# The last two slot tiles of two routed expert layers reach the tokens by matrix products instead of gathers

## The reference

```
# L1: top 2 of softmax + bias, with a shared expert beside
comb = sum_c weights[c] * one_hot(idx[c])               # [512, 8]
routed = sum_e comb[:, e] * (swiglu((x@w1[e]+b1[e]) * (x@w3[e]+b3[e])) @ w2[e] + b2[e])
out = routed + swiglu((x@sw1+sb1) * (x@sw3+sb3)) @ sw2 + sb2
# L2: top 2 of the logits, gates renormalised over the two, hidden width 1024
out = sum_e comb[:, e] * (relu(x@W1[e]+b1[e]) @ W2[e] + b2[e])
```

## Time and profile before

| | us |
|---|---|
| median of 3 timed runs | 2891.98 (2891.62 to 2898.47) |
| the profiled execution | 2884.38 |
| its span, first to last instruction | 2882.6 |
| TensorE busy | 2647.0 (92%) |
| VectorE (DVE) busy | 1643.5 (57%) |
| ScalarE (ACT) busy | 1114.2 (39%) |
| GpSimd (POOL) busy | 608.2 (21%) |
| routed layer of L1, in the span | 1956 to 2181 |
| routed layer of L2, in the span | 2353 to 2520 |

### The profile page before, as it was taken

One profiled execution on the slowest core, in us unless ns is written; L12 is line 12 of the kernel. 1 busy time (PEld: TensorE's weight loads), 2 busy tenths in 40 slices (PEclk: granted clock), 3 DMA queues, 4 the chain that ended last, 5 costly groups with the idle time before them and its releaser, 6 DMA issues. The chain is left out here.

```text
span 2882.6 us, 44108 instructions
## 1 busy us (share of the span) xinstructions
PE 2647.0 (92%) x17643; PEld 1856.3 (64%) x17643; DVE 1643.5 (57%) x3718; ACT 1114.2 (39%) x1997; POOL 608.2 (21%) x316
## 2 busy tenths in 40 slices
PE   6999999999999998689999888998997789799978
PEld 3666666666666666466767646775993458678846
DVE  5657666666667554646665556773552350177755
ACT  3343434434343432235555547651332443211123
POOL 2041312212140400000000005771001050145402
PEclk8999999999999999899999999998998999899989
DMA  5323333332334221221010001115767338543210
GB/s 172 105 76 97 86 97 99 79 104 72 102 80 109 63 60 26 111 86 53 28 43 24 2 7 38 45 38 197 301 251 277 132 123 311 186 173 137 69 37 15
DMA packets 91121, 296.06 MB, mean 103 GB/s; under 512 B 8944, under 2 KB 46518, under 8 KB 84006
## 3 DMA queue, kind: packets, MB, share of 16 engines
q1 hardware_dynamic: 86918, 284.27, 30.8%
q0 software_dynamic: 2976, 8.13, 0.8%
q10 hardware_dynamic: 1024, 0.86, 0.1%
HBM read 281.16 MB, written 11.54 MB: 102 GB/s over the span
## 5 line engine op out<-in xcount | busy, mean ns | idle before, releaser
L1962 PE MATMUL L_xattn_bank<-L_xattn_keys_tok,L_xattn_probsT 128*128 128x257 f32 x1664 | 412.9, 392 | 1.1 <-ACT L_xattn_probsT L1781 0.2
L1891 PE MATMUL L_xattn_wide<-L_xattn_keys_feat,weights_a 128*128 128x512 f32 (+2 forms) x1024 | 387.4, 521 | 6.5 <-ACT L_xattn_keys_feat L1801 3.6
L1962 PEld LDWEIGHTS L_xattn_bank<-L_xattn_keys_tok,L_xattn_probsT 128*128 128x128 f32 x1664 | 300.7, 190 | 91.3 <-issue 40.9
L1891 PEld LDWEIGHTS L_xattn_wide<-L_xattn_keys_feat,weights_a 128*128 128x128 f32 x1024 | 185.6, 191 | 153.8 <-issue 127.4
L1539 DVE COPY L_xattn_k_normed<-L_xattn_wide 128x833 f32<-128x833 f32 (+1 forms) x128 | 131.1, 1024 | 185.8 <-PE L_xattn_wide L1891 185.4
L1775 ACT ACTIVATE L_xattn_scores<-L_xattn_scores,L_xattn_neg_max 128x897 f32<-128x897 f32 x128 | 126.4, 1035 | 256.4 <-DVE L_xattn_neg_max L1564 256.4
L2940 DVE TENSOR_TENSOR_SCAN L_attn_state<-L_attn_decay,L_attn_banks 128x1024 f32<-128x1024 f32 x80 | 178.8, 2275 | 59.6 <-PE L_attn_banks L3146 59.6
L3050 POOL TENSOR_TENSOR L_attn_state<-L_attn_state,L_attn_C_rows 128x1024 f32<-128x1024 f32 x80 | 187.3, 2363 | 61.4 <-DVE L_attn_state L2940 61.4
L1559 DVE CUSTOM_DVE_ANT_0 L_xattn_scores<-L_xattn_wide,L_xattn_mask_row 128x897 f32<-128x897 f32 x128 | 134.9, 1088 | 105.2 <-issue 105.2
L2179 DVE CUSTOM_DVE_ANT_0 L_xattn_scores<-L_xattn_banks,L_xattn_mask 128x512 f32<-128x512 f32 (+1 forms) x256 | 131.4, 570 | 92.4 <-issue 92.4
L3146 PEld LDWEIGHTS L_attn_banks<-L_attn_B_diagonal,L_attn_dt_u_tok 128*128 128x128 f32 x1280 | 148.2, 194 | 38.0 <-issue 34.7
(11 more groups left out here) (530 smaller groups left out, 4685.3 us busy)
## 6 DMA issues: line engine op xcount, KB each, us to landing
L_xattn_k_scale<-L_xattn_k_scale_rows SPq DMA_DIRECT2D x128, 417.0 KB, 5.1
L_ffn_expert_w<-in_x_L_ffn SPq DMA_DIRECT2D x16, 2056.0 KB, 10.1
L_xattn_ctx_feat<-in_ctx_feat SPq DMA_DIRECT2D x19, 1601.0 KB, 9.7
L_ffn_expert_w<-in_x_L_ffn SPq DMA_DIRECT2D x17, 1024.0 KB, 5.5
L_ffn_expert_w<-in_x_L_ffn SPq DMA_DIRECT2D x15, 1028.0 KB, 5.7
L_xattn_keys_tok<-in_ctx_tok SPq DMA_DIRECT2D x8, 1536.0 KB
L_attn_C_rows<-L_attn_c_rows SPq DMA_DIRECT2D x48, 256.0 KB, 3.2
L_xattn_ctx_tok_and_one<-in_ctx_tok SPq DMA_DIRECT2D x8, 1536.0 KB
```

The costliest lines, as they stand in the source:

```text
L1891: last = nc.tensor.matmul(wide[:, 2 * h + c, 0:n], wk[:, k, p * P:(p + 1) * P], xnT[b % 2][:, k, a:a + n], start=(k == 0), stop=(k == KT - 1))
L1962: last = nc.tensor.matmul(bS[:, 0:D + 1], pT[:, c, a, :, :].rearrange("p h q -> p (h q)"), xn[b % 2][:, t, :], start=(i == 0), stop=(i == ...
```

## The change

`TAIL` = 2 and `CUT` = 13. Only tiles 0 to 12 are stored to `slots_y`, and the gathers wait for these 13 stores alone. They read at `near`, which is min(pos, 13 * 128 - 1), and the gate used with a gathered row is `near_gate`, which is zero where the choice's slot is in tile 13 or 14. For these two tiles a matrix of 128 tokens x 128 slots is made for each token group: the gate where the token's slot is that slot, zero elsewhere (`tail_gates`, DVE, tiles 2 to 5). TensorE turns them (`turn_tail`, after tiles 4 and 6), DVE copies them to SBUF (`tail_taken`, tiles 5 and 7), and TensorE multiplies them with the tile's result in `ysb` (`add_tail`), tile 13 before down(14) and tile 14 after it. DVE adds the two sums of two token groups each to x at the end. The pack of both layers gets 256 more columns, `slot_no`.

```diff
-                for j in range(TILES):
+                for j in range(CUT):
                     pool.wait_ge(y_ready, j + 1)
                     nc.gpsimd.dma_start(slots_y[j * P:(j + 1) * P, :], ysb[:, j % 3, :]).then_inc(y_stored[j % 3], 16)
                 for s in range(3):
-                    pool.wait_ge(y_stored[s], 16 * (TILES // 3) * (use + 1))
+                    pool.wait_ge(y_stored[s], 16 * STORES[s] * (use + 1))
+                pool.wait_ge(near_ready, 1)
                 for t in range(NT):
                     for c in range(2):
                         nc.gpsimd.indirect_dma_start(got[:, t, c, :], None, slots_y,
-                                                     bass.IndirectOffsetOnAxis(pos[:, c, t:t + 1], 0)
+                                                     bass.IndirectOffsetOnAxis(near[:, c, t:t + 1], 0)
...
+                def split_positions():
+                    dve.wait_ge(pos_ready, 1)
+                    chain(nc.vector.tensor_copy(pos_f[:, :, :], pos[:, :, :]))
+                    chain(nc.vector.tensor_scalar(near_f[:, :, :], pos_f[:, :, :], float(CUT * P - 1), None, ALU.min))
+                    nc.vector.tensor_copy(near[:, :, :], near_f[:, :, :]).then_inc(near_ready, 1)
+                    nc.vector.scalar_tensor_tensor(near_gate[:, :, :], pos_f[:, :, :], float(CUT * P), gate[:, :, :],
+                                                   ALU.is_lt, ALU.mult)
+                    chain(nc.vector.tensor_scalar(tail_slot[:, :, :], pos_f[:, :, :], -float(CUT * P), None, ALU.add))
+
+                def tail_gates(t):
+                    slot_no = w[:, at["slot_no"]:at["slot_no"] + TAIL * P]
+                    if t:
+                        dve.wait_ge(tail_ready, t)
+                    for c in range(2):
+                        last = nc.vector.tensor_scalar(tail_of[:, c, :], slot_no, tail_slot[:, c, t:t + 1], gate[:, c, t:t + 1],
+                                                       ALU.is_equal, ALU.mult)
+                    chain(last)
+                    nc.vector.tensor_tensor(tail[:, t, :, :].rearrange("p a n -> p (a n)"), tail_of[:, 0, :],
+                                            tail_of[:, 1, :], ALU.add).then_inc(tail_ready, 1)
+
+                def tail_taken(h):
+                    dve.wait_ge(tail_turned, h + 1)
+                    nc.vector.tensor_copy(tailT[:, :, 2 * h:2 * h + 2, :].rearrange("p a t n -> p t a n"),
+                                          ps[:, 7, :].rearrange("p (t a n) -> p t a n", t=2, n=P)).then_inc(tailT_ready, 1)
...
+                    if j == 1:
+                        split_positions()
+                    if 2 <= j < 2 + NT:
+                        tail_gates(j - 2)
+                    if j in (5, 7):
+                        tail_taken((j - 5) // 2)
...
-                        chain(nc.vector.scalar_tensor_tensor(L.x[:, t, :], got[:, t, c, :], gate[:, c, t:t + 1],
+                        chain(nc.vector.scalar_tensor_tensor(L.x[:, t, :], got[:, t, c, :], near_gate[:, c, t:t + 1],
                                                              L.x[:, t, :], ALU.mult, ALU.add))
+                for h in range(2):
+                    dve.wait_ge(tail_added, h + 1)
+                    nc.vector.tensor_tensor(L.x[:, 2 * h:2 * h + 2, :], L.x[:, 2 * h:2 * h + 2, :],
+                                            ps[:, 7 - h, :].rearrange("p (t n) -> p t n", n=D), ALU.add)
...
+                def turn_tail(h):
+                    pe.wait_ge(tail_ready, 2 * h + 2)
+                    if h:
+                        pe.wait_ge(tailT_ready, h)
+                    for t in (2 * h, 2 * h + 1):
+                        for a in range(TAIL):
+                            c = (t % 2 * TAIL + a) * P
+                            last = nc.tensor.transpose(ps[:, 7, c:c + P], tail[:, t, a, :], L.ident)
+                    last.then_inc(tail_turned, 1)
+
+                def add_tail(a):
+                    j = CUT + a
+                    pe.wait_ge(y_ready, j + 1)
+                    if a == 0:
+                        pe.wait_ge(tailT_ready, 2)
+                    for t in range(NT):
+                        last = nc.tensor.matmul(tail_bank(t), tailT[:, a, t, :], ysb[:, j % 3, :], start=(a == 0),
+                                                stop=(a == TAIL - 1), skip_group_check=True)
+                        if a == TAIL - 1 and t % 2:
+                            last.then_inc(tail_added, 1)
...
+                    if j in (4, 6):
+                        turn_tail((j - 4) // 2)
+                for h in range(TAIL - 1):
+                    add_tail(h)
                 down(TILES - 1)
+                add_tail(TAIL - 1)
```

More of the change, by code:

```diff
@@ L3256 @@
 TILES = 15
+TAIL = 2
 def route_vector(L, nc, dve, chain, T, logit_ps, counts_ps, w, at, kind, sems):
@@ L3338, in routed_experts @@
     G = MF // 2 if swiglu else MF // 4
+    CUT = TILES - TAIL
+    STORES = [len(range(s, CUT, 3)) for s in range(3)]
     use, L.routed_layers = L.routed_layers, L.routed_layers + 1
@@ L3351, in routed_experts @@
         slots_x = nc.dram_tensor(name + "slots_x", (TILES * P, D), F32, kind="Internal").ap()
-        slots_y = nc.dram_tensor(name + "slots_y", (TILES * P, D), F32, kind="Internal").ap()
+        slots_y = nc.dram_tensor(name + "slots_y", (CUT * P, D), F32, kind="Internal").ap()
         g3 = lambda n, dt=F32: sb(n, [P, NT, E], dt)
@@ L3363, in routed_experts @@
              sb("ended", [P, TILES, E]), sb("expert_f", [P, TILES]), own)
+        pos_f = sb("position_f", [P, 2, NT])
+        near_f = sb("near_position_f", [P, 2, NT])
+        near = sb("near_position", [P, 2, NT], U32)
+        near_gate = sb("near_gate", [P, 2, NT])
+        tail_slot = sb("tail_slot", [P, 2, NT])
+        tail_of = sb("tail_of_choice", [P, 2, TAIL * P])
+        tail = sb("tail_gates", [P, NT, TAIL, P])
+        tailT = sb("tail_gatesT", [P, TAIL, NT, P])
         combT = sb("combineT", [E, NT, P])
@@ L3414, in routed_experts @@
         y_gathered = L.y_gathered
+        near_ready = sem("near_ready")
+        tail_ready = sem("tail_ready")
+        tail_turned = sem("tail_turned")
+        tailT_ready = sem("tailT_ready")
+        tail_added = sem("tail_added")
         first_done = sem("first_done")
@@ L3440, in y_bank, with tail_bank @@
             return ps[:, 4 + j % 2, 0:D]
+        def tail_bank(t):
+            return ps[:, 7 - t // 2, (t % 2) * D:(t % 2 + 1) * D]
         def chunk_of(g, c):
@@ L3621, in stored @@
                     if j >= 3:
-                        act.wait_ge(y_stored[j % 3], 16 * (TILES // 3 * use + j // 3))
+                        act.wait_ge(y_stored[j % 3], 16 * (STORES[j % 3] * use + j // 3))
                     nc.scalar.activation(ysb[:, j % 3, :], y_bank(j), ACT.Copy).then_inc(y_ready, 1)
@@ L4048, in pack_routing @@
     k.add("tile_no", TILES, lambda i: _bc(np.arange(TILES, dtype=np.float32)))
+    k.add("slot_no", TAIL * P, lambda i: _bc(np.arange(TAIL * P, dtype=np.float32)))
 def pack_l0_attn():
```

## The result

| | before | after |
|---|---|---|
| median of 5 timed runs each, us | 2891.98 (2887.32 to 2898.47) | 2865.76 (2860.69 to 2868.35) |
| profiled execution, us | 2884.38 | 2865.76 |
| its span, us | 2882.6 | 2864.0 |

The ratio is 0.9909 with a 95% interval of 0.9895 to 0.9923, so 22 to 30 us off; 24.6 were forecast, and the median of 2865.8 stands beside a forecast of 2867.4.

A forecast was written before the change was run, and what follows sets the result against it. TensorE was taken to bound the tiles and a serial DVE and POOL chain the layers' ends. Gains of 12.9 in L1 and 11.7 in L2 make 24.6 us off the median 2891.98: 2867.4, range 2859 to 2876.

The forecast's parts named there:

- Bound and stage: Routed expert layers L1 and L2: TensorE bounds the tiles, a serial DVE and POOL chain the ends, priced from tile 12 on.
- Transposes, 0.9 a layer: After tiles 4 and 6, turn_tail's 8 transposes on a full TensorE shift all that follows by 0.9 us, range 0 to 1.5.
- DVE's work free in L1: Tiles 2 to 7 of L1: added DVE work delays the feature copy 0.4 to 1.1 us within 1.9 of slack, cost 0.
- The gathers' move: Layer ends: first gather 2.83 us after tile 12's store, last some 8.86 later, data 2.86 after that; L2's sums wait for it.
- L1's end: Gain at L1's end: 12.1 us if TensorE's clock falls before down(14), 13.7 if it stays up; middle 12.9 taken.
- add_tail: Around down(14): four products cost 0.9 to 1.0 us at full clock; tile 13's fit the gap before it, cost 0.
- the gain for L2: L2's end: the gathers are late, DVE is free at 2505.6, the layer ends at 2507.0, 11.7 us gained.
- Rival 1: Gathers land in 7.1 us instead of 2.86, L2's end moves by 4.3, L1's hardly: 2872 us; chance 0.08.
- Rival 2: In L1, POOL issues gathers only while DVE is idle, ending at 2168.7; 22.8 us off, 2869; chance 0.05.
- The factor of five: Estimate by the skill page's DVE-blocks-DMA trap: two or three gathers out before 2160.6, L1 ends about 2173, time some 2873 us.
- Rival 3: At the next layers' start TensorE's clock falls, losing 2.3 us at one or both boundaries: 2869.7 to 2872.0; chance 0.10.
- The signs named ahead: Last slot copy to next statistics becomes about 4.6 us in L1, 5.6 in L2; wrong if the next opening differs over 1.

The follow-up runs named there:

- e1: Against the kernel before, only the gathers moved behind tile 12's store, without gate matrices, products or last additions, tiles 13 and 14 left out of the output: 2862.91 us, ratio 0.9894.
- e2: Against the kernel before, only gate matrices, transposes, products and last additions added, with 15 stores and the gathers still behind tile 14's: ratio 1.0003.
- e10: The changed kernel with each tail_gates computing its masked rows three times over: 2868.39 us in one execution.
- e9: The changed kernel with POOL waiting for near_ready first, then the buffers' stores in the order 1, 2, 0: 2869.41 us in one execution.
- e3: The changed kernel with TAIL = 1: 14 stores, gathers behind tile 13's, one tile by products; ratio to the kernel before 0.9964.
- e7: The changed kernel with L1's first two token groups' accumulations done before hidden(14, 1): 2866.97 us in one execution.
- e5: The changed kernel run once more, unchanged: 2867.77 us, ratio to the kernel before 0.9916.
- e4: The changed kernel with tile 13's four products placed behind down(14) instead of before it: 2870.61 us in one execution.
- e11: The changed kernel with one unread product behind add_tail(1) and one more at the opening of L2's and L3's cross-attention: ratio to the kernel before 0.9905.

## Why the prediction was right

- **Bound and stage.** Right: TensorE full among the tiles, and the gain wholly in the ends. e1 and e2 take it apart.
- **Transposes, 0.9 a layer.** 0.87 in both layers.
- **DVE's work free in L1.** Right, with its reason confirmed (e10). The slack was 1.82 us, as read (1.9), and the changed kernel left 1.45 of it at the tightest tile, more than the 0.8 that the prediction's 1.9 less 1.1 gives, with the transposes as cover that it didn't count. Two tensor_scalars with per-partition operands took 0.73, as priced (2 x 0.36).
- **The gathers' move.** L1: 8.88 us between the first and the last gather's start, all landed before DVE wanted them. L2: as worked out, but begun 2.26 us after the store and not 2.83, since another buffer's wait blocks (e9).
- **L1's end.** Of the two cases, 12.1 and 13.7, it was the second: clock up, and DVE's own work last, level with TensorE's. 14.88 - 0.87 = 14.0. The middle, 12.9, was the hedge that cost 1.1.
- **add_tail was mis-sized.** The prediction priced its four products at "0.9 to 1.0", from 3.69 us for 16. Those 16 are instructions in the trace, and each float32 product of this kind is two of them: down has 8 products in L2 and shows x16. add_tail took 1.89 to 1.99 us. The error was hidden. In L1 the four of tile 13 still fit into the gap, which shrank to 1.57 instead of 2.2 (that this made the clock surer to stay up is likely and not shown). In L2 they didn't fit into the 1.28 us before down(14), which the prediction priced at 0 "with some 0.3 to spare": down(14) starts 9.88 us after tile 12's store and not 9.59. With that and the longer add_tail(1), TensorE came out level with the gathers (0.25 us late), where the prediction had it 0.8 ahead, and this ate nearly half of the 0.57 gained by the earlier gather. So the gain for L2, 11.96 against 11.7, is met in part by two errors that cancel.
- **Rival 1 (late landing)** did not come: 2.7 to 2.9 us to landing for every gather of the traces read for it (before, after, e1, e3, e7, e9), clamped rows or not.
- **Rival 2 (DVE holds POOL)** did not come in the changed kernel, whose gathers beside DVE take 0.95 to 1.02. Single gathers beside DVE in e1, e3, e7 and e9 took 1.05 to 1.20 us, so there one or two gathers in eight were held up by 0.1 to 0.25 us each. The factor of five of the Trainium skill's page "SBUF — State Buffer" (section "SBUF: two separate sides") did not show: the longest gather of all traces took 1.20 us, where they take 0.94 to 1.02 alone; see the last section.
- **Rival 3 (the next layers' clock)** came true in mechanism at both boundaries, at a price of 0 and 1.6 us of the two layers' lengths. One of the prediction's own signs of being wrong came with it: the opening of L2's cross-attention takes 10.5 us against 9.1, more than the 1 us allowed. The reason given for taking 0, that the opening chain waits for DVE and ACT at either level, leaves out the first products behind that chain, which took 5.10 us and not 3.67. The fall was given 0.10, and both traces of the changed kernel have it twice. The 3.9 us of L2's scan layer, one layer on, are clock too, and the prediction has no term for them. Whether the change brings them about stays open: 25.97 less 3.9 is 22.1, about the lower edge of the 22 to 30 measured.
- **The signs named ahead.** From the last slot copy to the next layer's statistics it is 4.42 us in L1 and 4.64 in L2 (4.6 and 5.6 forecast). The tail additions of L1 didn't wait for TensorE, which ended level with DVE. The one sign of being wrong that came is the opening above.
- **Sum.** 25.97 by the layers' fixed lengths, 26.2 by the medians (22.8 by those of e5, run beside other executions of the kernel before), 24.6 forecast. The main terms and the path were right. That L2 alone comes within 0.3 us is luck in part, by the errors that cancel there; the middle taken in L1 cost 1.1.

## What to carry to other kernels

When a serial chain ends a stage (store, wait, gather, add), look for the last pieces of work that needn't go through it; give them a way of their own, and the chain runs beside them. Take as many pieces as it needs for the other ends to come level, and no more: with one tile the gathers were the bound, with two DVE and TensorE end together in L1 and the gathers and TensorE in L2, and early sums gained nothing. When pricing a matmul from a row, find out how many of its instructions make one product.

## What the runs showed of the hardware

- POOL starts the DMA behind a row of waits some 0.5 us sooner if the wait that blocks is the first of them: 2.22 to 2.38 us from the store (after, e1, e4, e10, e11), against 2.74 and 2.75 with the second of four blocking (e3), 2.83, 2.80 with the last of three (before), 2.88, 2.87 with the third of four (e2) and 2.79, 2.78 with the last of four (e9).
- POOL's gathers and DVE hold each other up a little, and not always. A tensor_scalar of 128x256 takes 0.28 us, and 0.42 to 0.43 in two of the changed kernel's L1 that start 0.63 to 0.65 us into a gather; one that starts 0.44 into a gather takes 0.28:

```profile
2154.42 0.97 POOL L3527 DMA_INDIRECT L_ffn_gathered<-L_ffn_slots_y,L_ffn_near_position  x1 [0.30 <-issue]
2155.07 0.43 DVE L3580 TENSOR_SCALAR L_ffn_gate_linear<-L_ffn_gate_linear 128x256 f32<-128x256 f32 x1
...
2158.21 0.95 POOL L3527 DMA_INDIRECT L_ffn_gathered<-L_ffn_slots_y,L_ffn_near_position  x1 [0.30 <-issue]
2158.65 0.28 DVE L3580 TENSOR_SCALAR L_ffn_gate_linear<-L_ffn_gate_linear 128x256 f32<-128x256 f32 x1
...
2158.84 0.42 DVE L3583 TENSOR_SCALAR L_ffn_gate_linear<-L_ffn_gate_linear 128x256 f32<-128x256 f32 x1
```

- The other way round, a gather that starts 0.10 to 0.14 us after a scalar_tensor_tensor or tensor_tensor of 128x256 took 1.11 to 1.20 us instead of 0.95 (one each in e1, e3, e7 and e9). The longest is e7's:

```profile
2161.90 2.04 DVE L3625 SCALAR_TENSOR_TENSOR x_tok<-L_ffn_gathered,L_ffn_near_gate,x_tok 128x256 f32<-128x256 f32 x4
...
2163.56 1.20 POOL L3527 DMA_INDIRECT L_ffn_gathered<-L_ffn_slots_y,L_ffn_near_position  x1 [0.30 <-issue]
```

- The same idle stretch of 3.30 us before the same product ended at either clock, in the middle of it, or left it up. Layers that none of the kernels touches differ by 2.6 to 5.2 us between profiled executions, along with the time that TensorE's clock is at half in them: L0's self-attention takes 52.3 us with the clock up in its first 10 us and 54.9 with 6.8 of them at half; L2's scan layer takes 86.1 to 86.3 us with 10.2 us at half and 89.0 to 91.3 with 17 to 24. The run-to-run spread is of this order.
